# Graph attention: a running sum kept on TensorE, and one folded by VectorE two bodies later

## What is computed

```python
q = (nfeat @ Wq.T).reshape(n, HEADS, HEAD_DIM) / SCALING     # HEADS 8, HEAD_DIM 32
k = (nfeat @ Wk.T).reshape(n, HEADS, HEAD_DIM)
v = (nfeat @ Wv.T).reshape(n, HEADS, HEAD_DIM)
attn = jnp.einsum('ehd,ehd->eh', k[src], q[dst]) + attn_bias
m = jax.ops.segment_max(attn, dst, num_segments=n)
a = jnp.exp(attn - m[dst])
s = jax.ops.segment_sum(a, dst, num_segments=n)
out = jax.ops.segment_sum(v[src] * (a / s[dst])[:, :, None], dst, num_segments=n)
```

## Time and profile before

| | us |
|---|---|
| median of 3 runs | 4670.8 (4656.6 to 4671.4) |
| span of the profiled execution | 4655.4 |
| attention stage in it, first L2100 to last L2016 | 236.1 to 1760.9 |
| PE, DVE, ACT, POOL busy in the span | 3057.1, 2425.4, 1172.9, 1430.1 |

### The profile page before, as it was taken

How to read it: one execution, slowest core, us unless ns; L and a number is a source line. 1 busy time by engine, 2 the same in 40 slices (tenths; PEclk the granted TensorE clock), 3 DMA queues, 4 the chain that set the end, 5 groups by cost and what they waited for, 6 DMA issues and landing times. The chain is left out here.

```text
span 4655.4 us, 51661 instructions
## 1 busy us (share of the span) xinstructions
PE 3057.1 (66%) x15437; PEld 2518.7 (54%) x15437; DVE 2425.4 (52%) x4153; ACT 1172.9 (25%) x2479; POOL 1430.1 (31%) x1393
## 2 busy tenths in 40 slices
PE   4234444444444445486688885999975996499698
PEld 2123333333333334364588884777755885388587
DVE  7446556666666664443699984111134665323333
ACT  1111111111111111121255552333323552000122
POOL 4655555555555552544340000000000000001133
PEclk8667777777777777598799995999987998699799
DMA  2556555555655655244254444000017443455333
GB/s 88 157 173 173 170 170 170 170 168 172 174 169 167 177 161 199 85 69 88 78 211 168 172 171 146 12 11 11 6 57 150 140 133 104 174 204 176 124 65 54
DMA packets 289833, 613.00 MB, mean 132 GB/s; under 512 B 52204, under 2 KB 195696, under 8 KB 279760
## 3 DMA queue, kind: packets, MB, share of 16 engines
q0 software_dynamic: 105584, 294.01, 23.3%
q1 hardware_dynamic: 166800, 267.12, 16.7%
q10 hardware_dynamic: 17360, 50.80, 3.7%
HBM read 437.46 MB, written 176.95 MB: 132 GB/s over the span
## 5 line engine op out<-in xcount | busy, mean ns | idle before, releaser
L2052 PE MATMUL gnn_p_msg<-gnn_msg,gnn_ident 128*128 128x264 f32 x2088 | 670.8, 491 | 933.9 <-issue 778.3
L2052 PEld LDWEIGHTS gnn_p_msg<-gnn_msg,gnn_ident 128*128 128x128 f32 x2088 | 508.6, 249 | 1096.0 <-issue 805.7
L1996 POOL DMA_INDIRECT gnn_got<-kv,gnn_index x928 | 879.9, 948 | 628.7 <-DVE gnn_msg L2111 358.5
L2492 PE MATMUL tables_p_pair<-tables_spread,tables_hot 128*128 128x100 f32 x3328 | 395.6, 278 | 18.7 <-DVE tables_spread L2466 17.0
L2492 PEld LDWEIGHTS tables_p_pair<-tables_spread,tables_hot 128*128 128x128 f32 x3328 | 380.8, 193 | 32.9 <-DVE tables_spread L2466 29.9
L2117 DVE TENSOR_TENSOR gnn_msg<-gnn_p_msg,gnn_keep 128x264 f32<-128x264 f32 x116 | 49.6, 428 | 516.9 <-DMA front_w<-in_L_gnn_Wq 401.7
L2773 PE MATMUL gnn_p_sum<-gnn_hs,gnn_edge 128*128 x2500 | 289.4, 279 | 32.4 <-DVE gnn_edge L2803 31.9
L2773 PEld LDWEIGHTS gnn_p_sum<-gnn_hs,gnn_edge 128*128 128x128 f32 x2500 | 286.6, 195 | 36.4 <-issue 35.9
L2100 DVE TENSOR_TENSOR gnn_prod<-gnn_got,gnn_p_q 128x2048 f32<-128x2048 f32 x116 | 265.4, 2288 | 66.5 <-issue 34.7
L1141 PE MATMUL ffn_pA<-ffn_hw,ffn_slabs 128*128 128x256 f32 x1250 | 274.8, 382 | 33.5 <-DMA ffn_beta<-in_L_ffn_beta 33.5
L737 DVE SCALAR_TENSOR_TENSOR ffn_acc<-ffn_pC,ffn_gates,ffn_acc 128x256 f32<-128x256 f32 x200 | 88.9, 480 | 395.3 <-PE ffn_pC L588 395.3
(11 more groups left out here) (413 smaller groups left out, 4808.9 us busy)
## 6 DMA issues: line engine op xcount, KB each, us to landing
weight_table<-tables_weight_slab SPq DMA_DIRECT2D x13, 3200.0 KB
count_table<-tables_count_row SPq DMA_DIRECT2D x13, 3200.0 KB
ffn_slabs<-weight_table SPq DMA_DIRECT2D x25, 1600.0 KB
gnn_cell<-count_table ACTq DMA_DIRECT2D x50, 576.0 KB, 3.7
state<-gnn_out SPq DMA_DIRECT2D x116, 136.0 KB
ffn_xs<-by_expert SPq DMA_DIRECT2D x60, 260.0 KB, 3.3
gnn_got<-kv,gnn_index POOLq DMA_INDIRECT x928
ffn_x<-x SPq DMA_DIRECT2D x20, 640.0 KB, 5.4
```

The source lines that it names most:

```text
L1996: pool.indirect_dma_start(out=got[k][:, r, :], out_offset=None, in_=kv_dram, in_offset=rows_at(index[k][:, r:r + 1])).then_inc(gathered[k] ...
L2052: last = nc.tensor.matmul(p_msg[v][:, 0:MSG], ident[:], msg[v][:, r].rearrange("p h d -> p (h d)"), start=(r == 0), stop=(r == R))
L2492: last = nc.tensor.matmul(at, hot[c % AHEAD][:, r, :], spread[c % AHEAD][:, r, :], start=True, stop=True)
```

## The change

PE adds only the eight rows of a body, into a ring of four PSUM banks, `p_msg[k]`. The ninth row is gone. The running sum lives in `out[k]` in SBUF, a ring of four: DVE computes out[b] = out[b-1] x keep[b] + p_msg[b] in a new function `merge`, with one multiply and one add, for body b-2 at the end of body b (LAG = 2). `merge` waits for `summed` and sets `out_ready`. `msg`, `keep` and `out` become rings of four; `peak[k]` is the tail of `out[k]`, so ACT's copy of it (L2034) is gone, as is ACT's copy of the sum (L2016). DVE waits for `keep_ready` and `stored` ahead of the maximum. PE waits for `released[k]` and `keep_ready` instead of `messages_ready` and `out_ready`. `p_q` and `p_weight` of a body share one bank. After the loop DVE folds the last two bodies. The plan's DVE code clears ten small tiles in place of one.

```diff
+LAG = 2
-        msg = [s.sb(f"msg{v}", [P, R + 1, HEADS, HD + 1]) for v in range(2)]
+        msg = [s.sb(f"msg{k}", [P, R, HEADS, HD + 1]) for k in range(SETS)]
-        peak = [s.sb(f"peak{v}", [P, HEADS]) for v in range(2)]
-        keep = [s.sb(f"keep{v}", [P, HEADS]) for v in range(2)]
-        out = [s.sb(f"out{v}", [P, STATE]) for v in range(2)]
+        keep = [s.sb(f"keep{k}", [P, HEADS]) for k in range(SETS)]
+        out = [s.sb(f"out{k}", [P, STATE]) for k in range(SETS)]
+        peak = [out[k][:, MSG:STATE] for k in range(SETS)]
-        p_msg = [s.ps(f"p_msg{v}", [P, 512]) for v in range(2)]
-        p_weight = [s.ps(f"p_weight{v}", [P, 512]) for v in range(2)]
-        p_q = [s.ps(f"p_q{v}", [P, 512]) for v in range(2)]
+        p_msg = [s.ps(f"p_msg{k}", [P, 512]) for k in range(SETS)]
+        p_both = [s.ps(f"p_both{v}", [P, 512]) for v in range(2)]
+        p_q = [p_both[v][:, 0:F] for v in range(2)]
+        p_weight = [p_both[v][:, F:F + R * HEADS] for v in range(2)]
...
-                        act.wait_ge(stored, 16 * b + 16)
-                        act.activation(out[v][:, MSG:STATE], peak[v][:], ACT.Copy)
                         stage(b + 1, 1 - v)
                         find_index(b + SETS, k)
-                        act.wait_ge(messages_ready, b + 1)
-                        copy_sum(1 - v)
...
-                        pe.wait_ge(messages_ready, b + 1)
-                        pe.wait_ge(out_ready, b + 1)
-                        for r in range(R + 1):
-                            last = nc.tensor.matmul(p_msg[v][:, 0:MSG], ident[:],
+                        pe.wait_ge(released[k], g + 2)
+                        pe.wait_ge(keep_ready, b + 2)
+                        for r in range(R):
+                            last = nc.tensor.matmul(p_msg[k][:, 0:MSG], ident[:],
...
+                def merge(k, count):
+
+                    of = out[k % SETS]
+                    dve.wait_ge(summed, count)
+                    dve.tensor_tensor(by_head(of), by_head(out[(k - 1) % SETS]),
+                                      over(keep[k % SETS][:], [P, HEADS, HD + 1], "p (h a) -> p h a", a=1), ALU.mult)
+                    dve.drain()
+                    dve.tensor_tensor(of[:, 0:MSG], of[:, 0:MSG], p_msg[k % SETS][:, 0:MSG], ALU.add)
+                    dve.drain().then_inc(out_ready, 1)
...
+                        dve.wait_ge(keep_ready, b + 1)
+                        dve.wait_ge(stored, 16 * b + 16)
+                        dve.tensor_reduce(peak[k], score[v][:].rearrange("p r h -> p h r"), AX.X, ALU.max)
...
-                        dve.wait_ge(keep_ready, b + 1)
-                        dve.wait_ge(summed, b + 1)
-                        dve.tensor_tensor(msg[v][:, R, :, :], p_msg[1 - v][:, 0:MSG].rearrange("p (h d) -> p h d", h=HEADS),
-                                          over(keep[v][:], [P, HEADS, HD + 1], "p (h a) -> p h a", a=1), ALU.mult)
-                        dve.drain().then_inc(messages_ready, 1)
+                        merge(k - LAG, b + 1)
+                total = group_count(dve) * SETS
+                for late in range(LAG):
+                    merge(late - LAG, total + (late + 1))
```

53 lines of the change are left out of this document (27 added, 26 removed).

## The result

| | before | changed |
|---|---|---|
| median, us | 4668.5 | 4490.8 (4477.3 to 4495.3) |
| ratio | | 0.9614, interval 0.9593 to 0.9635 |
| span of the profiled execution | 4655.4 | 4475.8 |
| end of the attention stage in it | 1760.9 | 1584.95 |

The change takes 3.9% off. The stage ends 176 us earlier, and what follows it takes 2890.9 us where it took 2894.5, so the 179.6 us of the span are nearly all this stage's.

The account below looks back on a forecast made before the run. Bound taken: PE's sums late during gathers, DVE waiting for them, POOL for DVE. From 4655.4, 48 us less for shorter cycles and 2 more for the last bodies gave 4609; plus 15.4, 4625. Own range 4560 to 4655; 8-in-10 range 4330 to 4763.

Parts of the forecast that it names:

- The bound: Attention stage: PE's sum is late while gathers run, DVE waits for the sum, POOL for DVE; 13.01 us a body.
- DVE per body: A multiply and an add replace L2117, so a body without waits grows from 8.51 to 9.0 us.
- two new waits ahead of the maximum: DVE's waits for `keep_ready` and `stored` ahead of L2106: allowed 0 to 1 us for the store, taken as 0.
- multiply with two SBUF operands: The fold's multiply on DVE while POOL prepares gathers: contention priced at nothing, since L2108 ran in 0.23 us.
- PE per body: PE's sum has 16 records for 18; a late sum takes 19.1 to 21.5 us, taken as 20.
- The new cycle: Attention stage: a late sum holds up PE's next; five bodies in 63 us, 12.6 a body, 48 us less.
- second late sum: PE's sum straight after a late one: 35.2 us in the earlier trace, taken as 25 in the forecast.
- case of no change: Rival: sums straight after a late one take 26 to 28 us, giving 4660 to 4690; chance 0.13.
- ACT's edits: ACT loses L2016 (0.39 us) and an 8-column copy (0.19 us), neither ahead of a DVE wait: nothing.
- Overlap rival: PE issues the next sum during a late completion, DVE hardly waits, POOL bounds: 355 us less, 4316; chance 0.20.
- No change in the surroundings: Nine more memsets before `plan_ready`, hidden (2.5 us if uncovered), and `p_q` and `p_weight` sharing a bank: nothing.

Follow-up runs that it names:

- e2: The changed kernel with DVE adding message rows 4 to 7 onto rows 0 to 3 before PE sums four rows; 4501.9 us, ratio 0.9582.
- b1_serial: The changed kernel with one more wait: PE starts a sum only when the sum of the body before is complete; 4592.3 us, ratio 0.9807.
- a1: The changed kernel with ACT writing the index list of body b+4 before staging the query and bias of body b+1; 4590.6 us, ratio 0.9809.
- d3: The changed kernel with twelve rows in each sum instead of eight, 24 matmul records a body for 16; 4639.5 us, ratio 0.9871.
- e3: The changed kernel with each row summed in two halves of 132 columns, twice the PE instructions, same columns and output; 4691.8 us, ratio 0.9985.
- d4: The changed kernel gathering 1 KB rows from the queries' table instead of 2 KB rows of keys and values; 4505.1 us, ratio 0.9628.
- e1: The changed kernel with messages and identity matrix stored as bf16, 8 matmuls and 8 weight loads a body; 4488.8 us, ratio 0.9554.
- f2: The changed kernel with bf16 messages, and index list, queries and bias column moved from ACT to DVE; 4549.9 us, ratio 0.9681.
- a2: The changed kernel with the fold's lag raised from two bodies to three, on chip B; 4277.0 us, ratio 1.0007 to the kernel before there.

## Why the prediction was wrong, step by step

*The bound.* Right where sums are late, as they are in the earlier trace rows: DVE behind the sum, POOL behind DVE. What the trace of before could not say is that this is not so on every chip.

*DVE per body.* 9.0 us foreseen, 9.12 measured. Most of the difference are the two new waits ahead of the maximum, priced at 0: 19.6 us in all ahead of L2118, 0.17 a body, where L2106 had the 0.07 of its drain. The multiply with two SBUF operands takes 429 ns, as long as L2117 with one operand in PSUM (428), so DVE pays nothing, as the 0.23 us of the earlier trace rows had said. But POOL pays, a price that the prediction put at nothing. The gather at 937.97, beside the multiply at 937.89, takes 1.16 us and not 0.95, and the next starts 1.47 us after it and not 1.25. Of the 928 gathers of the changed kernel 25 take over 0.98 us, each of them beside L2095, 4.9 us in all; the kernel before has none. In e2, whose pair add has two SBUF operands for 1.26 us, POOL's mean gather is longer; the first row is the changed kernel's, the second e2's, 240 to 1560 us:

```profile
L1998 POOL DMA_INDIRECT gnn_got<-kv,gnn_index x915 | 869.8, 951 | 436.4 <-issue 271.9 <-ACT gnn_index L2008 148.0 <-DVE gnn_msg L2123 16.5
L1999 POOL DMA_INDIRECT gnn_got<-kv,gnn_index x912 | 926.6, 1016 | 394.4 <-issue 294.3 <-ACT gnn_index L2009 99.5 <-DVE gnn_msg L2123 0.6
```

The Trainium skill ("SBUF — State Buffer", Who interferes with whom), cited in the prediction, states such a contention between a VectorE instruction with two SBUF inputs and GpSimd's reads. The trace agrees, with POOL as the one that takes longer, some 0.2 us at a time.

*PE per body.* A late sum of 20 us, then one of 25: b1_serial has 17.6 and 19.0 in one pair, 17.0 and 23.2 in the next. As terms they were about right.

*The new cycle: the step that failed.* "PE starts the sum of b+2 at 29" takes it that PE stands until a late sum is complete. The changed kernel starts it 9 us after the one before and at full pace, at 938.10, when the sum of 928.99 is still 18 us from its completion. I had the row for it, PE's records at full pace in 6.85 us, and set against it the second late sum of the earlier trace rows. But in that kernel PE was bound to wait for DVE's fold, which stood behind the sum. The sequence of 24.5 and 35.2 us came from the program's own wait and from the length of that run of gathers, 46 us by then. It said nothing of whether PE could go ahead. What b1_serial adds to the changed kernel, 0.9807 against 0.9614, is the price of this step: 1.9%, some 90 us. The part of the miss from 4592 to 4625 is that b1_serial's bodies took 12.3 us on average (79 us less than the kernel before over 116 bodies), and not 12.6. Two of the prediction's bounds are also a few us off by its own steps: a second late sum of 21.8 us gives some 4555 and not 4560, and its case of no change runs from about 4650 to 4695 and not from 4660 to 4690. Nothing hangs on that.

*The cycle that came instead.* Four bodies in 45.65 us, 32 gathers, one fold wait of 8.60 us and one POOL wait of 5.7. Foreseen were five bodies, 40 gathers and a wait of over 15. I had asked what is late next of PE alone; late next was ACT, whose index list ends each run after 32 gathers (148.0 us, 29 times). That I had put ACT's edits at nothing was right for the two instructions it lost, and left out the seven it kept. Writing the list earlier doesn't help: a1 takes away most of this wait and loses 91 us, since the query is later in its place.

*Overlap rival (chance 0.20).* Its mechanism was right and its time, 4316, was not: it took overlap to mean that DVE hardly waits, but half of the wait is left, because the hold-up isn't a fixed delay of 20 us. As the rows of d3 suggest, with starts 2.1 to 2.8 us apart, it is a rate, by which what follows gets later the longer the run goes on.

*No change in the surroundings.* The nine memsets and the shared bank cost nothing that the traces show: PE's first sum starts at 243.68, where it started at 244.48.

## What is shown, what is argued

Shown: on four of five chips, and on the chip of the first comparison, instructions of engines other than POOL are late within a run of gathers; the lateness of TensorE's goes by their number (e3, and d3 with it) and not by their columns (e3) or the bytes gathered (d4), and a low clock doesn't bring it (e1); it moves from engine to engine (e1, f2); on one chip it isn't there for either kernel.

Argued only: what holds them up. The steps of 0.70 us look like a queue that takes one entry in that time, as long as gathers are being issued, and into which each engine puts entries for each instruction. No run changed the number of gathers. The fetching of instructions is hardly the cause: from 240 to 1380 us, the queue for instructions moved two packets in the changed kernel, as many as in a2 on chip B:

```profile
q14 instruction: 2, 0.02, 0.0%
```

One candidate is the writing of the trace's own records. The Trainium skill ("NOTIFIC — the notification-queue block", "Overflow: three behaviours, one of which stalls the engine") says that the block which writes such records holds back rather than lose one inside it, and that a count of stalls would mean that this path had slowed an engine. The traces would fit that, with engines slowed by their number of records and not by their work. The same page has a measured rate of at least 6.6 million records a second without loss, far above one in 0.70 us, and nothing here shows why it should be lower while POOL gathers, nor on some chips only. No run here could take the records away, so it stays open whether the kernels differ by 3.9% when none are written.

## What to carry to other kernels

When one engine waits for another's late completion, ask first whether the late engine is itself held by a wait in the program: the same lateness costs a whole sum each time if the next one must wait for it, and only the excess over the lag if not. Then look for the engine that is late next under the same cause; here TensorE, ScalarE and VectorE took turns, and halving the instructions of one bought under 1%. And take a comparison on more than one chip before believing in a gain that comes from hiding a delay which no line of the program explains.

## What the runs showed of the hardware

- The same program takes 4275 us on one chip and 4671 to 4706 on four others, at an equal or nearly equal granted clock (0.75 and 0.72 in the stage); the difference lies in the attention stage, which in a2 on that chip ends at 1406 us, where the kernel before ends it at 1761 on a slower one: 355 of the 378 us between their spans.
- On the slower chips instructions that wait for nothing start 6 us and more late within a run of gathers, in steps of 0.70 us; PE goes on issuing at full pace for three sums before it is held (919.88, 928.99, 938.10; the fourth, at 947.68, breaks after ten records).
- POOL's gather of 128 rows takes 1.25 us to issue on every chip, with rows of 2 KB or of 1 KB.
- Halving the number of PE's instructions with bf16 messages takes the fold's wait from 256.8 us to 0.0 and leaves the time within 1% of the changed kernel's ratio (0.9554 against 0.9614 and 0.9628).
- A VectorE instruction with both inputs in SBUF lengthens the gather that POOL issues beside it: 1.16 us for 0.95 beside the fold's multiply, and a mean of 1016 ns for 951 in e2. VectorE's own time doesn't change (429 ns).
